# Expert layer 2: tokens of the first three groups come first in the block table, and their sums are made beside the last thirteen blocks

## The reference, cut to what matters

```python
g = softmax(h @ Wr)                     # h: layer norm of x; 8 experts, 4096 tokens
top2_w, top2_idx = top_k(g, 2); top2_w = top2_w / sum(top2_w)
hid = relu(einsum('bsh,ehf->bsef', h, W1))           # 128 -> 512
expert_out = einsum('bsef,efh->bseh', hid, W2)       # 512 -> 128
x = x + sum(take(expert_out, top2_idx) * top2_w, axis=2)
```

## Time and profile before

| | us |
|---|---|
| median of three runs (988.32 to 990.34) | 988.71 |
| span of the profiled execution (first to last instruction) | 993.1 |
| PE busy in that span | 926.8 |
| DVE busy | 544.1 |
| ACT busy | 543.1 |
| POOL busy | 365.3 |

### The profile page before, as it was taken

How to read it: one execution, slowest core, us unless ns; L and a number is a source line. 1 busy time by engine, 2 the same in 40 slices (tenths; PEclk the granted TensorE clock), 3 DMA queues, 4 the chain that set the end, 5 groups by cost and what they waited for, 6 DMA issues and landing times.

```text
span 993.1 us, 31589 instructions
## 1 busy us (share of the span) xinstructions
PE 926.8 (93%) x11919; PEld 693.9 (70%) x11919; DVE 544.1 (55%) x1934; ACT 543.1 (55%) x1082; POOL 365.3 (37%) x387
## 2 busy tenths in 40 slices
PE   7999999999999999969998899999999999999990
PEld 6446655664689999965544594577458589999990
DVE  5236455355476532207579648767786787861104
ACT  2543343325305555536766666775678476666760
POOL 2300412321234776543140112122432345777760
PEclk9999999999999999989999999999999999999995
DMA  8744314403403233213020120120015513133316
GB/s 220 225 88 86 70 48 100 108 24 89 105 28 82 77 96 94 64 60 129 3 87 3 51 83 1 46 89 16 22 55 162 163 30 82 56 98 96 105 37 254
DMA packets 78260, 82.77 MB, mean 83 GB/s; under 512 B 12207, under 2 KB 60164, under 8 KB 77600
## 3 DMA queue, kind: packets, MB, share of 16 engines
q1 hardware_dynamic: 64128, 58.29, 22.3%
q0 software_dynamic: 10176, 19.04, 6.2%
q10 hardware_dynamic: 3808, 3.41, 1.1%
HBM read 53.96 MB, written 27.64 MB: 82 GB/s over the span
## 4 chain that ended last, share of the span: by engine, by line
PE 32%; DVE 11%; issue 4%; DMA 3%; ACT 3%; SPq 1%; POOL 1%; DVEq 0%; POOLq 0%; ACTq 0%
PE b_ring L1802 8%; PE b_ring L1745 4%; PE b_g L1851 4%; PE b_g L1824 4%; PE b_ring L1303 4%; PE b_ring L1314 4%; PE b_ring L1866 2%; DVE b_kq L2221 2%; ACT early L1979 1%; DMA early<-expert_parts 1%; DVE x L1391 1%; DVE b_prod L2130 1%; ACT b_outT L1991 1%; DVE b_coef L2133 1%; PE b_s L1811 1%
## 5 line engine op out<-in xcount | busy, mean ns | idle before, releaser
L1802 PE MATMUL b_ring<-b_hT,b_qkT 128*128 128x512 f32 x256 | 119.9, 607 | 6.0 <-DVE b_kq L2221 4.6
L2221 DVE SCALAR_TENSOR_TENSOR b_kq<-b_exp,b_ring 128x512 f32<-128x512 f32 x128 | 83.3, 683 | 40.2 <-ACT b_exp L1959 38.6
L276 POOL DMA_INDIRECT expert_rows<-f_route_sent,f_route_place_id x64 | 62.9, 982 | 97.4 <-DVE f_route_place_id L232 50.8
L1959 ACT ACTIVATE b_exp<-b_ring 128x512 f32<-128x512 f32 x128 | 73.8, 603 | 31.5 <-PE b_ring L1802 21.6
L1802 PEld LDWEIGHTS b_ring<-b_hT,b_qkT 128*128 128x128 f32 x256 | 45.3, 189 | 61.3 <-issue 41.0
L982 ACT ACTIVATE phik<-a_ring 128x512 f32<-128x512 f32 x64 | 38.2, 597 | 81.4 <-PE a_ring L825 81.4
L276 POOL DMA_INDIRECT expert_rows<-g_route_sent,g_route_place_id x48 | 50.0, 1041 | 83.7 <-PE b_ring L1866 36.9
L1303 PE MATMUL b_ring<-b_v,b_kq 128*128 128x128 f32 x568 | 75.3, 276 | 0.6 <-issue 0.4
L1303 PE MATMUL a_ring<-phik 128*128 128x128 f32 x568 | 75.0, 275 | 0.4 <-ACT phik L1324 0.4
L1314 PE MATMUL b_ring<-wide,b_v 128*128 x568 | 75.1, 276 | 0.0
L1314 PE MATMUL a_wide<-wide,phiqT 128*128 x568 | 74.7, 275 | 0.0
(11 more groups left out here) (332 smaller groups left out, 1838.2 us busy)
## 6 DMA issues: line engine op xcount, KB each, us to landing
a_rn_wide<-norm_compact SPq DMA_DIRECT2D x28, 512.0 KB, 8.4
wide<-in_L_ffn_W SPq DMA_DIRECT2D x32, 256.0 KB, 5.4
early<-expert_parts SPq DMA_DIRECT2D x12, 512.0 KB, 5.9
a_rn_wide<-expert_rows SPq DMA_DIRECT2D x71, 65.0 KB
b_coef<-gram_compact SPq DMA_DIRECT2D x4, 1024.0 KB, 4.9
b_hT<-expert_rows SPq DMA_DIRECT2D x56, 65.0 KB
x<-in_L_attn_a_x SPq DMA_DIRECT2D x8, 256.0 KB, 4.0
gram_compact<-wide SPq DMA_DIRECT2D x32, 64.0 KB
```

The source lines that it names most:

```text
L276: pool.indirect_dma_start(self.rows, bass.IndirectOffsetOnAxis(self.place_id[:, k, n:n + 1], 0), self.sent[:, n, k, :], None).then_inc(sel ...
L1802: pe.matmul(ring[n % 4][:, :], w, hT[:, g % 2, half * 512:half * 512 + 512], start=True, stop=True)\
L1959: act.activation(exps[:, n % EXPS, :], ring[n % 4][:, :], ACT.Exp, bias=-1.0).then_inc(S["exp_ready"], 1)
L2221: dve.scalar_tensor_tensor(out=kq[:, p % 2, half:half + FOURS // 2, slot:slot + T * FOUR], in0=exps[:, n % EXPS, :].rearrange("p (a n) -> ...
```

## The change

Three things are changed.

1. **The table is ranked.** When rounds 0 to 5 have been placed (at DVE's j = 11, right before the second phase) a new step `mark` notes, for each expert, how many rows lie in whole blocks and how many in touched blocks at that point. The third and fourth phases then work with 16 entries in place of 8: first what is left of the marked rows of each expert, then the rest. Masks and scratch areas grow to match. With this, blocks 0 to 56 (`B_EARLY` = 49 + 8) hold all rows of groups 0 to 2.
2. **The sums are split.** After the last fetch, SP waits until the scatters of blocks 0 to 56 have landed (by pairs, thus 57 too), loads the parts of groups 0 to 2 in four DMAs of two batches (768 KB each) into free areas, DVE adds them at j = 63, 65, 67 and 69 (after `take` of that j), and SP stores each result (384 KB). Only group 3 is left for the end: four loads of 256 KB, two issued by SP and two by ACT, eight adds of 128 x 256, four stores of 128 KB, SP and ACT in turn.
3. **POOL's scatters** from block 33 on are paced a little earlier.

The diff, cut to its core:

```diff
+B_EARLY = B_FULL[2] + EXPERTS
 class BlockTable:
+    def entries(self, phase):
+        return 2 * EXPERTS if phase in self.ranked else EXPERTS
...
+    def rows_of(self, dve, out, partial):
+        n, shift = TOKENS // P, self.shift_all[:, 0:EXPERTS]
+        self.then(dve, dve.scalar_tensor_tensor(out=shift, in0=self.C["filled"][:, :],
+                                                scalar=0.0 if partial else -float(P - 1),
+                                                in1=self.C["regions"][:, :], op0=ALU.add, op1=ALU.subtract))
+        self.then(dve, dve.tensor_tensor(self.past_full, shift.unsqueeze(1).to_broadcast([P, n, EXPERTS]),
+                                         self.C["block_rows"][:, 0:n].unsqueeze(2).to_broadcast([P, n, EXPERTS]), ALU.is_gt))
+        self.then(dve, dve.tensor_reduce(out, self.past_full.rearrange("p b e -> p e b"), AX_X, ALU.add))
+        self.then(dve, dve.tensor_scalar(out, out, float(P), None, ALU.mult))
+    def mark(self, dve):
+        self.rows_of(dve, self.whole, False)
+        self.rows_of(dve, self.touched, True)
     def count(self, dve, phase, last):
...
+        if phase in self.ranked:
+            first, second = self.n_all[:, 0:EXPERTS], self.n_all[:, EXPERTS:2 * EXPERTS]
+            self.then(dve, dve.tensor_tensor(first, self.touched if last else self.whole, self.used, ALU.subtract))
+            self.then(dve, dve.tensor_scalar(first, first, 0.0, None, ALU.max))
+            self.then(dve, dve.tensor_tensor(second, self.n_blocks, first, ALU.subtract))
     def limits(self, dve, phase, lo):
+        m = self.entries(phase)
+        self.then(dve, dve.tensor_tensor(upto, n_rows.unsqueeze(1).to_broadcast([P, m + 1, m]),
+                                         self.C["below"][:, 0:m + 1, 0:m], ALU.mult))
+        self.then(dve, dve.tensor_reduce(ends, upto, AX_X, ALU.add))
     def experts(self, dve, phase, lo, hi):
+        if phase in self.ranked:
+            self.then(dve, dve.scalar_tensor_tensor(out=table, in0=past[:, :, EXPERTS], scalar=-float(EXPERTS), in1=table,
+                                                    op0=ALU.mult, op1=ALU.add))
     def starts(self, dve, phase, lo, hi, last):
+        for o in range(0, m, EXPERTS):
+            ins = dve.scalar_tensor_tensor(out=shift[:, o:o + EXPERTS], ...)
+        if phase:
+            for o in range(0, m, EXPERTS):
+                ins = dve.tensor_tensor(shift[:, o:o + EXPERTS], shift[:, o:o + EXPERTS], self.used, ALU.add)
+        if phase in self.ranked:
+            self.then(dve, dve.tensor_tensor(shift[:, EXPERTS:m], shift[:, EXPERTS:m], self.n_all[:, 0:EXPERTS], ALU.add))
...
+            for o in range(0, m, EXPERTS):       # not in the last phase
+                self.then(dve, dve.tensor_tensor(self.used, self.used, taken, ALU.add))
+                self.then(dve, dve.tensor_tensor(self.used, self.used, begins, ALU.subtract))
 AttentionWeights.tables (DVE, start of the kernel)
-        for e in range(1, EXPERTS + 1):
+        for e in range(1, 2 * EXPERTS + 1):
             dve.memset(C["below"][:, e, 0:e], 1.0)
 class FinalSum:
+    EARLY = NT - 1
+    EARLY_PARTS = LATE_PARTS = 4
+    EACH = BATCH // EARLY_PARTS
+    def load_early(self, sp):
+        for i in range(self.EARLY_PARTS):
+            sp.dma_start(self.early[i], self.parts.rearrange("(t p g k) c -> p t (g k c)", k=2, t=BATCH, p=P)
+                         [:, self.batches(i), 0:self.EARLY * 2 * DIM]).then_inc(self.part_in[i], 16)
+    def add_early(self, dve, i):
+        dve.wait_ge(self.part_in[i], 48)
+        for k in range(2):
+            dve.tensor_tensor(self.x_early(i), self.x_early(i), part[:, :, :, k, :], ALU.add).then_inc(self.sum_step, 1)
+    def store_early(self, sp):
+        for i in range(self.EARLY_PARTS):
+            sp.wait_ge(self.sum_step, 2 * i + 2)
+            sp.dma_start(self.out...[:, self.batches(i), 0:self.EARLY, :], self.x_early(i))
+    def load_late(self, eng, which):
+        eng.wait_ge(self.sum_step, 2 * self.EARLY_PARTS)
+        for i in which:
+            eng.dma_start(self.late[:, self.batches(i), :], self.parts...[NT - 1, :, self.batches(i), :])
+    def add_late(self, dve): ...
+    def store_late(self, eng, which): ...
 sync
+            ffn.stored_before(sp, B_EARLY)
+            sp.wait_ge(S["x_ready"], NG)
+            final.load_early(sp)
+            final.store_early(sp)
             ffn.stored(sp)
-            final.load(sp)
+            final.load_late(sp, (0, 2))
+            final.store_late(sp, (0, 2))
+            final.all_stored(sp)
 gpsimd
             for k in range(BLOCKS - j):
-                ffn.begun(pool, b + k * (BLOCKS - 1 - b) // (BLOCKS - 1 - j))
+                ffn.begun(pool, max(b + 2 * k // 3, j + k - 1))
                 ffn.scatter(pool, j + k)
 scalar
-            final.store(act)
+            ffn.stored(act)
+            final.load_late(act, (1, 3))
+            final.store_late(act, (1, 3))
 vector
+            SUMS_AT = BLOCKS - 2 * FinalSum.EARLY_PARTS
...
                 elif j == 11:
+                    block_table.mark(dve)
                     block_table.part(dve, 1, 0)
...
-            final.add(dve)
+                elif j >= SUMS_AT and (j - SUMS_AT) % 2 == 0:
+                    final.add_early(dve, (j - SUMS_AT) // 2)
+            final.add_late(dve)
```

More of the change, by code:

```diff
@@ L344, in part @@
         last = phase == len(self.bounds) - 1
[L345 removed]
         if i == 0:
[L347 removed]
+            self.count(dve, phase, last)
         elif i == 1:
@@ L366, in count @@
+    def mark(self, dve):
+        self.rows_of(dve, self.whole, False)
+        self.rows_of(dve, self.touched, True)
+    def count(self, dve, phase, last):
+        if last:
+            dve.tensor_copy(self.C["tail"][:, :], self.C["filled"][:, :]).then_inc(self.tail_ready, 1)
+        self.rows_of(dve, self.n_blocks, last)
         if phase:
             self.then(dve, dve.tensor_tensor(self.n_blocks, self.n_blocks, self.used, ALU.subtract))
[L369 to L373 removed]
+        if phase in self.ranked:
[3 more added lines that the diff above has]
+            self.then(dve, dve.tensor_tensor(second, self.n_blocks, first, ALU.subtract))
```

153 lines of the change are left out of this document (79 added, 74 removed).

## The result

| | before | changed |
|---|---|---|
| median, us | 989.53 (988.32 to 990.72, 4 runs) | 983.23 (982.65 to 984.82, 4 runs) |
| span of the profiled execution, us | 993.1 | 980.9 |
| granted clock, mean of that execution | 0.976 | 0.989 |

The ratio is 0.9926, with a 95% interval of [0.9904, 0.9947]: 6.3 us less by the medians, where 5.8 were forecast (982.9, range 976.8 to 986.4).

What follows compares the result with a forecast made beforehand. Transfers bound the 20.5 us end, and in the middle PE is at its peak only because DVE is just in time. Table +5.6, early sums 0, late sums −11.4 give −5.8: 988.7 to 982.9 us, range 976.8 to 986.4.

Steps and rivals of the forecast that it cites:

- The table's price, 5.6 us: Middle: 8.4 us of added DVE table work, partly hidden, makes PE 5.6 us late to the end; bounds 4.5 and 7.
- Where PE waits: Middle: PE waits for DVE at blocks 28 to 32; `take` of block 30 has 0.1 us of slack.
- The early sums cost nothing: Before the end: early loads, adds and stores stay hidden, with 4 us to spare before `take` of block 70.
- rival E: Near the end: `take` of block 70 stuck behind the first early add, making the kernel slower; chance 0.06.
- rival D: End: early traffic still under way when the last scatter lands, likeliest loss 2 to 5 us, 985 to 988; chance 0.09.
- The late sums, 9.1 in place of 20.5: End, from the first late load: 9.1 us in place of 20.5, 11.4 us saved; bounds 10 and 12.
- The sum: Whole kernel: 5.6 − 11.4 = −5.8 us, on the median 988.7 − 5.8 = 982.9.
- The clock: PE: by the skill's rule every new pause could be paid twice; the sum has nothing for it.
- rival C: Middle: the delay is larger, through a slow clock (1.7 or 3.4 us) or slow steps, 984.6 to 987; chance 0.11.
- POOL's pace: Scatters of blocks 34 on move by up to one block; nothing at the end.

Runs made afterwards that it cites:

- Experiment 1: Only the ranked table added to the kernel before, with its old end and POOL's old pace; 993.82 us against 989.35, ratio 1.0048.
- experiment 2: The changed kernel with `mark` executed twice; 985.81 us, ratio 0.9963 to the kernel before.
- experiment 8: The kernel before once more, no edit, timed and traced; 991.98 us, ratio 1.0009, span 986.9 us.
- experiment 5: The changed kernel with the fillers' copy right after round 7 is placed and fourth-phase parts at j = 26, 28, 30, 32; 980.35 us against 990.89, ratio 0.9896.
- Experiments 9: The changed kernel with PE's register reads for blocks 66 to 70 made eight blocks earlier; 1048.85 us against 1060.47 for the kernel before, ratio 0.986.
- experiment 12: The changed kernel with a shorter marking, moved table parts and the last five register reads eight blocks earlier; 979.79 us against 990.65 for the kernel before, ratio 0.9879.
- experiment 4: The kernel before once more, no edit, for a second trace; one execution of 995.01 us, span 993.3 us.
- experiment 6: The changed kernel with POOL's old pace of scatters; 984.3 us, ratio 0.9917 to the kernel before.

## Why the prediction was right, and where it was off

**The table's price, 5.6 us.** Right in size and in mechanism. Aligned, L359 of before is at 876.01 and its counterpart L384 at 881.64: 5.63. The parts agree too: the two row counts of the marking took 1.51 and 1.75 us (1.51 each and one slow step were priced), and a step on 374 elements 0.55. Block 30 starts 885.38 − 879.07 = 6.3 late (6.1 forecast), block 32 6.9 (6.6), the turn that had waited, in front of block 35, 895.90 − 890.54 = 5.4 (5.6), and block 66 955.40 − 949.65 = 5.75. Experiment 1 has 4.7 [3.1 to 6.3] for it as a time and 5.6 at block 66, experiment 2 the one-for-one. The aligned times rest on the shift of 6.92 between two traces; against experiment 8's trace it is 5.7 without any shift (118.78 − 113.06).

**Where PE waits.** Half right. I had it wait at `take` of blocks 28 to 32 and gave the window 2.6 us of false room; but 3.6 of its 7.2 us of waits come earlier, at the routings, for the same DVE. The sum didn't need the place, but a remedy does: experiment 5 shows that moving the fourth phase behind block 30's `take` is enough for most of it, and that this left the routings' waits as they were.

**The early sums cost nothing.** The step that failed, by about 1 us. Loads were issued at 949.93, 951.3 + 5.6 − 6.9 = 950.0 forecast; `take` of block 70 ran between the adds at 957.71, far from late (rival E had it there); the transfers were over before the late loads (rival D): the DMA engines move 0 GB/s from 968 to 970 us, and the first late load is issued at 972.04. But I had priced only DVE and the 16 DMA engines, and not the register reads of PE's own queue while the early stores run: three of the last five take 0.78 to 0.98 us in place of 0.30, and the stretch from block 66 on is 1.7 us longer, of which 1.0 reaches the last scatter (6.7 late where PE was 5.75 late; the rest is taken up by POOL, which started its last scatter 2.0 us after PE's end before, at 969.82 after 967.82, and 1.3 after it now, at 969.62 after 968.34). The windows of the changed kernel (columns of the earlier trace rows) show the load on the DMA engines there:

```profile
884.00:886.00 2.00, 0.62 (x5) 0.65 (x6) 1.19 (x4) 0.00 (x0) 0.56 (x1) 1.00 0.43 111
...
955.00:958.00 3.00, 3.00 (x30) 3.00 (x29) 2.12 (x3) 1.98 (x6) 1.77 (x2) 1.00 1.04 415
962.00:964.00 2.00, 2.00 (x19) 1.85 (x18) 1.72 (x3) 1.00 (x3) 1.36 (x2) 1.00 0.81 291
```

Experiments 9 and 12 put it to the register reads. In the window from 955 to 958, the busiest, the reads still take 0.30 us; the long ones begin at 958.89, after the first early store.

**The late sums, 9.1 in place of 20.5.** Right: 8.86 us from the first late load, and the load is issued 0.33 us after the last scatter has landed where it was 0.67, so 12.0 in all against 11.4, at the upper bound that I had given.

**The sum.** Forecast 5.6 + 0 − 11.4 = −5.8. By the traces 5.75 + 1.0 − 12.0 = −5.3, by the medians −6.3, by the ratio −7.3 (5.2 to 9.5). Two errors of 0.6 to 1.0 us with opposite signs stand in it, so that the total comes out closer than its terms is luck; a sum that comes out is no proof of each term.

**The clock.** The windows above show it at 1.00 around the new wait of 2.41 us, so at the upper of its levels, and PE's next hidden layer took 1.13 us. The Trainium skill ("TensorE: Matmul & The Clock Gate", Part 1), by which I held rival C open, has the throttled clock as the default that activity lifts. No new pause of the changed kernel, up to 2.41 us, was followed by a lower clock; this is in line with the 1.19 us of the earlier trace rows and unlike the 3.10 of the earlier trace rows. It isn't the length of the wait alone that decides, for in experiment 4 one of 1.99 us had a clock of 0.50 behind it. So the prediction's argument against rival C, that 1.19 us cost nothing, came out right here without being a safe one.

**POOL's pace.** No effect that the times resolve (experiment 6).

## What to carry to other kernels

An engine that reads as 74% busy can still have no room: look at how long before its consumer each of its results is ready, and price added steps against the smallest of those slacks; then move the added steps behind it, which here gave back 3.7 of 5.75 us before any step was made cheaper. A tail that is bound by transfers is worth splitting as soon as part of its input is final early, even at a price in the middle. Work that is "hidden" beside a busy engine should be checked for everything that this engine's queue reads, registers too, not for its data alone.

## What the runs showed of the hardware

- A register read of PE takes 0.30 us (median of 142, the longest 0.48, in the kernel before) and fits under the 0.9 us of matmuls in front of it (24 matmuls with two reads between them in 2.87 us). In the changed kernel three of the five reads behind the first early store take 0.78 to 0.98 us, the other two 0.30, and output layers start late; the longest pause is 0.67 us, in experiment 6. Early loads alone, at 361 to 415 GB/s, leave it at 0.30. That the pauses vanish with the reads is shown (15 of 15); why the stores make a read long is not.
- A second read in a block of 1.89 us costs PE 0.3 us even ahead of that traffic (the blocks from 942.23 and 944.40; the first early load is issued at 946.67), and 1.6 us in five blocks, though it stands behind matmuls as well. The first such block, from 940.33, costs nothing.
- The same program, the kernel before, had 989 and 1060 us in different groups. In the profiles of that group PE, ACT and DVE have gaps of up to 6 us. Their cause stays open.
- The long wait for DVE near 790 us came in two of three traces of the kernel before (3.10 and 2.7 us) and also in experiment 12 (2.93, at 790.70), a version of the changed kernel. So it goes with the execution and not with the kernel; what triggers it is open. Each time a low clock stood behind it (0.50 from 796 to 798 us in experiment 4). The windows of experiment 12 (columns of the earlier trace rows):

```profile
790.00:792.00 2.00, 1.30 (x49) 1.33 (x53) 1.76 (x10) 0.00 (x0) 0.00 (x0) 0.68 0.03 8
792.00:794.00 2.00, 2.00 (x87) 2.00 (x83) 1.83 (x8) 1.07 (x2) 0.00 (x0) 0.50 0.00 0
```

  So waits of 1.99 (experiment 4, in layer 2), 2.7, 2.93 and 3.10 us had a granted clock of 0.5 behind them, 1.2 GHz, and the one of 2.41 us at block 30 hadn't. The length of the wait doesn't separate the two kinds; what does is open.
